# A decoder block on one core: value projection moved to the start, context rows and row parts moved forward

## The reference

```python
x = layernorm(x + self_attention(x))      # 32 heads of 16, ALiBi, causal; w_attn 512 x 1536, w_proj 512 x 512
x = layernorm(x + cross_attention(x, ctx))  # 32 query heads, 8 key heads of 128; keys and values from [ctx; x]
x = layernorm(x + ffn(x))                 # a permutation, 16 blocks of 32 -> 128 -> 32, the permutation back

qkv = x @ w_attn + b_attn                 # self-attention
scores = q @ k.T / 16 + slope[h] * (key - query), causal
out = softmax(scores) @ v @ w_proj + b_proj

k, v = kv @ Wk, kv @ Wv                   # cross-attention: 512 -> 8 x 128, kv = concat(ctx, x), then
q, k = rms_norm(q) * q_norm_w, rms_norm(k) * k_norm_w
```

## Time and profile before

| | |
|---|---|
| median of 3 runs | 845.17 us (844.33 to 846.02) |
| profiled execution, its own time | 845.65 us |
| its span, first to last instruction | 843.8 us |
| TensorE products busy | 826.2 us, 98% |
| VectorE busy | 547.2 us, 65% |
| ScalarE busy | 474.9 us, 56% |
| GpSimd busy | 521.9 us, 62% |
| granted TensorE clock, mean | 0.999 |
| DMA | 56.22 MB, mean 67 GB/s |

### The profile page before, as it was taken

The page is one execution under the profiler, slowest core; times in us unless marked ns, Lnnn a source line. Parts: engine busy times, 40 slices in busy tenths (PEclk is TensorE's granted clock), DMA queues, the critical chain, the costliest instruction groups (busy, mean ns, idle before and its releaser), DMA issues.

```text
span 843.8 us, 15130 instructions
## 1 busy us (share of the span) xinstructions
PE 826.2 (98%) x4851; PEld 694.6 (82%) x4851; DVE 547.2 (65%) x1507; ACT 474.9 (56%) x1006; POOL 521.9 (62%) x676
## 2 busy tenths in 40 slices
PE   7999999999999999999999999999999999999997
PEld 5777777777788888888888888888888888888874
DVE  4456566766355677667767676667666766677664
ACT  4666665566246656455555555556555555556554
POOL 3477876757336576766666756775676576636931
PEclk9999999999999999999999999999999999999999
DMA  6613223221141721112102112122121101100101
GB/s 202 197 51 113 80 72 114 63 72 56 50 138 51 243 80 46 51 60 67 50 19 87 27 61 68 37 68 68 37 68 68 37 2 24 58 0 1 26 1 50
DMA packets 48511, 56.22 MB, mean 67 GB/s; under 512 B 4671, under 2 KB 29773, under 8 KB 48461
## 3 DMA queue, kind: packets, MB, share of 16 engines
q1 hardware_dynamic: 48460, 55.59, 21.6%
HBM read 41.95 MB, written 13.63 MB: 66 GB/s over the span
## 4 chain that ended last, share of the span: by engine, by line
PE 61%; DVE 3%; ACT 2%; POOL 0%; issue 0%; POOLq 0%
PE bank L1534 15%; PE bank L48 11%; PE bank L50 11%; PE bank L49 11%; PE bank L1580 9%; PE bank L1524 1%; ACT prob L1349 1%; DVE x_mx L1420 1%; ACT prob L1724 1%; DVE pT_lo L1469 0%; PE bank L1849 0%; PE bank L1850 0%; PE bank L1881 0%; PE bank L1891 0%; PE bank L1890 0%
## 5 line engine op out<-in xcount | busy, mean ns | idle before, releaser
L1251 POOL TENSOR_SCALAR prob<-prob,x_rinv 128x768 f32<-128x768 f32 x124 | 112.5, 908 | 167.4 <-DVE x_rinv L1429 167.4
L1366 ACT ACTIVATE pT_hi<-bank 128x512 fp32r<-128x512 f32 x192 | 114.2, 597 | 90.3 <-PE bank L1580 89.9
L1349 ACT ACTIVATE prob<-bank,x_nm,q_rms 128x768 f32<-128x768 f32 x124 | 123.2, 994 | 47.1 <-DVE x_nm L1423 46.7
L1469 DVE TENSOR_TENSOR pT_lo<-bank,pT_hi 128x512 fp32r<-128x512 f32 x192 | 130.3, 679 | 5.1 <-ACT pT_hi L1366 3.7
L1420 DVE TENSOR_REDUCE x_mx<-bank 128x1 f32<-128x768 f32 x124 | 118.3, 954 | 22.0 <-PE bank L1534 21.7
L1580 PE MATMUL bank<-ident,prob 128*128 128x128 f32 x768 | 114.8, 272 | 2.1 <-POOL prob L1251 1.3
L1580 PEld LDWEIGHTS bank<-ident,prob 128*128 128x128 f32 x768 | 95.0, 140 | 14.1 <-POOL prob L1251 2.0
L48 PE MATMUL bank<-pT_hi,xv_hi 128*128 128x512 f32 x192 | 86.5, 450 | 1.2 <-DVE pT_lo L1469 0.9
L485 ACT ACTIVATE s_self<-s_self,nm_self 128x128 f32<-128x128 f32 (+1 forms) x128 | 57.1, 447 | 43.0 <-DVE nm_self L628 42.5
L50 PE MATMUL bank<-pT_hi,xv_lo 128*128 128x512 f32 x192 | 75.7, 394 | 0.0
L49 PE MATMUL bank<-pT_lo,xv_hi 128*128 128x512 f32 x192 | 75.4, 393 | 0.0
(11 more groups left out here) (233 smaller groups left out, 2047.8 us busy)
## 6 DMA issues: line engine op xcount, KB each, us to landing
wo_raw<-in_Wo SPq DMA_DIRECT2D x8, 1024.0 KB, 5.4
v_by_head<-v_st SPq DMA_DIRECT2D x12, 512.0 KB, 3.5
kT_by_head<-kT_st SPq DMA_DIRECT2D x12, 512.0 KB, 3.2
xk_raw<-kT_by_head SPq DMA_DIRECT2D x16, 384.0 KB, 3.2
xv_raw<-v_by_head SPq DMA_DIRECT2D x16, 384.0 KB, 3.2
wq_raw<-in_Wq SPq DMA_DIRECT2D x6, 1024.0 KB, 5.5
wq_raw<-in_w_attn SPq DMA_DIRECT2D x12, 256.0 KB, 4.3
xk_raw<-in_ctx SPq DMA_DIRECT2D x8, 256.0 KB, 2.6
```

Source lines behind the costliest of these rows:

```text
L1251: nc.gpsimd.tensor_scalar(prob[:, s, :], prob[:, s, :], rinv[:, s:s + 1], 1.0, ALU.mult, ALU.mult)\
L1349: nc.scalar.activation(prob[:, s, :].rearrange("p (a e) -> p a e", a=2), bank[:, at:at + 2, 0:HALF], ACT.Exp, bias=nm[:, s:s + 1], scale=q ...
L1366: nc.scalar.activation(pT_hi[:, a, :], bank[:, turn.bank[s, what, a], :], ACT.Copy)\
L1469: nc.vector.tensor_tensor(pT_lo[:, a, :], bank[:, turn.bank[s, what, a], :], f32(pT_hi[:, a, :]), ALU.subtract).then_inc(ring_out, 1)
```

## The change

1. Loads alternate: row group 0, weight block 0, row group 1 and so on; the first weight group is now the values' (`w_attn` 2), then queries, keys.
2. The values are projected first, in the fixed part, in groups of three products between the row transposes; queries and keys follow. V leaves the order list. The first context rows are loaded earlier and transposed into bank 1 between queries and keys.
3. Groups 3 and 5 are split by VectorE instead of GpSimd (8 subtractions); ScalarE's and VectorE's splits of groups 2 to 5 are placed one by one between queries and keys.
4. The first four row parts go beside the scores of quad 0, and four cycles (c = 1, 3, 5, 7) have one part less. So up to S(9) every CT, KT and KG sits at another place than before.

```diff
-    order = [("S", 0), ("W", 5), ("V", 0), ("E", (0, 0)), ("V", 1), ("E", (0, 1)), ("V", 2), ("E", (0, 2)), ("CT", 0), ("CX", 0), ("V", 3),
-             ("E", (0, 3)), ("R", (0, 0)), ("W", 6), ("R", (0, 1))]
+    order = [("S", 0)]
...
+    for i in range(QUAD):
+        parts(1)
+        order.append(("E", (0, i)))
+        if i % 2:
+            order.append(("R", (0, i // 2)))
+    order.append(("W", 6))
...
-        if c < NQ - 1:
+        if c not in (1, 3, 5, 7, NQ - 1):
             parts(1)
...
-        ON_VECTOR, ON_POOL = (0, 1, 2, 4, 6, 8), (3, 5, 7)
+        ON_VECTOR, ON_POOL = (0, 1, 2, 3, 4, 5, 6, 8), (7,)
...
-        before = {4: ("V", 0), 7: ("V", 3), 5: ("V", 1), 6: ("V", 2)}
-        place, quad, rows_over = {}, 0, {}
+        before = {4: ("K", 0), 7: ("K", 3), 5: ("K", 1), 6: ("K", 2)}
+        place, quad, rows_over = {("CT", 0): (1, None)}, 0, {}
...
-                name, g = (("w_attn", 0), ("w_attn", 1), ("w_attn", 2), ("Wk", 0), ("Wk", 1), ("Wv", 0), ("Wv", 1),
+                name, g = (("w_attn", 2), ("w_attn", 0), ("w_attn", 1), ("Wk", 0), ("Wk", 1), ("Wv", 0), ("Wv", 1),
                            ("w_proj", 0), ("Wq", 0), ("Wq", 1))[p]
                 for i in range(KT):
-                    if p > 0 and p - 1 in ON_VECTOR:
+                    if p == 0:
+                        sp.dma_start(x[:, i, :], d["x"].rearrange("b s d -> (b s) d")[tokens(i), :]).then_inc(x_in[i], 16)
+                    elif p - 1 in ON_VECTOR:
                         sp.wait_ge(w_los, KT * ON_VECTOR.index(p - 1) + i + 1)
...
             load_weights(1)
             sp.dma_start(proj_bias, d["b_proj"].rearrange("(a n) -> a n", a=1).to_broadcast([P, D])).then_inc(proj_bias_in, 16)
+            load_context(0)
             load_weights(2)
-            load_context(0)
...
-            late_lo(3)
-            late_lo(5)
...
+            for i in range(KT):
+                weights_hi(2, i)
+            queries_of(0)
+            queries_of(1)
+            weights_hi(3, 0)
+            weights_hi(3, 1)
+            queries_of(2)
+            weights_hi(3, 2)
+            weights_hi(3, 3)
+            weights_hi(4, 0)
+            queries_of(3)
+            context_hi(0)
+            for i in range(1, KT):
+                weights_hi(4, i)
+            act.wait_ge(nw_made, 2)
+            keys_of(0)
+            weights_hi(5, 0)
+            weights_hi(5, 1)
+            keys_of(1)
+            weights_hi(5, 2)
+            weights_hi(5, 3)
+            keys_of(2)
+            keys_of(3)
...
+            def values(i, j):
+
+                pe.wait_ge(xt_lo, j + 1)
+                pe.wait_ge(w_los, i + 1)
+                last = three_passes(nc, bank[:, 4 + j, :], xT_hi[:, i, tokens(j)], xT_lo[:, i, tokens(j)],
+                                    w_hi[:, 0, i, :], w_lo[:, 0, i, :], i == 0, i == KT - 1)
+                if i == KT - 1:
+                    last.then_inc(v_ps, 1)
+
+            pe.wait_ge(const, 4)
+            row_transposes(0)
+            row_transposes(1)
+            values(0, 0)
+            row_transposes(2)
+            for i, j in ((0, 1), (1, 0), (1, 1)):
+                values(i, j)
+            row_transposes(3)
+            for i, j in ((0, 2), (1, 2), (2, 0), (2, 1), (2, 2), (0, 3), (1, 3), (2, 3)):
+                values(i, j)
+            for j in range(TT):
+                values(KT - 1, j)
```

More of the change, by code:

```diff
@@ L536, in _, with keys_of @@
                     .then_inc(q_out, 1)
[L537 to L541, removed]
+            def keys_of(m):
                 act.wait_ge(qk_ps, KT + m + 1)
@@ L544, in _ @@
                                      scale=even[:]).then_inc(k_out, 1)
-                weights_hi(4, m)
-            act.wait_ge(zeros, 2)
-            for what, a in ORDER:
[L548 to L555, removed]
+            for i in range(KT):
[21 more added lines that the diff above has]
+            keys_of(3)
+            for what, a in ORDER:
+                if what == "CX":
                     context_hi(a)
@@ L676, in _, with odd_keys @@
                                         f32(xT_hi[:, :, tokens(j)]), ALU.subtract).then_inc(xt_lo, 1)
-            for p in range(2):
-                for i in range(KT):
-                    early_lo(p, i)
+                early_lo(0, j)
+            for i in range(KT):
+                early_lo(1, i)
+            def odd_keys(m):
+                dve.wait_ge(qk_ps, KT + m + 1)
+                dve.wait_ge(k_out, m + 1)
+                nc.vector.tensor_scalar(kT_odd[:, m, :], bank[:, 4 + m, :], cols[:, KT + m:KT + m + 1],
+                                        odd[:], ALU.add, ALU.mult).then_inc(k_odd_out, 1)
+            for i in range(KT):
+                early_lo(2, i)
             dve.wait_ge(col_out, 1)
@@ L685, in _ @@
             for i in range(KT):
[L686 to L692, removed]
+                early_lo(3, i)
+            early_lo(4, 0)
+            context_lo(0)
+            for i in range(1, KT):
+                early_lo(4, i)
+            odd_keys(0)
+            early_lo(5, 0)
+            early_lo(5, 1)
+            odd_keys(1)
+            early_lo(5, 2)
+            early_lo(5, 3)
+            odd_keys(2)
+            odd_keys(3)
             for what, a in ORDER:
@@ L796, in drained, with context_transposes, row_transposes @@
                     pe.wait_ge(vg_late, i[0] + 1)
-            pe.wait_ge(const, 4)
-            for j in range(TT):
+            def context_transposes(n):
+                pe.wait_ge(c_in, 16 * (n + 1))
+                if n > 0:
+                    drained("CT", n)
+                for i in range(KT):
+                    last = nc.tensor.transpose(bank[:, bank_of("CT", n), tokens(i)], c_raw[:, tokens(i)], ident[:])
+                last.then_inc(ct_ps, 1)
+            def row_transposes(j):
                 pe.wait_ge(x_in[j], 16)
@@ L870, in weigh_values @@
                 last.then_inc(o_ps, 1)
-            def context_transposes(n):
-                pe.wait_ge(c_in, 16 * (n + 1))
-                drained("CT", n)
-                for i in range(KT):
-                    last = nc.tensor.transpose(bank[:, bank_of("CT", n), tokens(i)], c_raw[:, tokens(i)], ident[:])
-                last.then_inc(ct_ps, 1)
             def key_transposes(n, g):
@@ L912, in _ @@
             for what, a in ORDER:
-                if what == "V":
-                    values(a)
-                elif what == "S":
+                if what == "S":
                     scores(a)
@@ L947, in _ @@
                         pe.wait_ge(s_out, QUAD * NQ)
[L948 removed]
+                        pe.wait_ge(w_los, 8 * KT)
                     for i in range(KT):
```

69 lines of the change are left out of this document (34 added, 35 removed).

## The result

The change makes the kernel slower: 852.42 us median of 4 executions (851.74 to 852.55), against 844.75 us for the kernel before in the same rounds (843.11 to 846.02). The ratio is 1.0083, with a 95% interval of 1.0071 to 1.0096. The profiled execution took 851.74 us with a span of 849.9 us, 6.1 more than before. Forecast were 848.6 us (844.0 to 851.2): the direction was right, the loss was more than twice what I summed, and the time lies outside the range.

What follows compares the result with a forecast made beforehand. TensorE was taken as the bound. A lead of -2.3 us, old waits gone at -1.9 and new waits of +7.7 gave +3.5 on the median of 845.17: 848.6 us, range 844.0 to 851.2.

Steps and rivals of the forecast that it cites:

- T(2,0): Transposes of quad 2's head 0: TensorE waits 2.7 us for VectorE's late result of the weighed values.
- S(5): Scores of quad 5: TensorE waits 1.1 us for a shift that VectorE makes after a context copy.
- T(4,2) with T(4,3): Transposes of quad 4's heads 2 and 3: waits of 2.3 us in all, behind GpSimd's late weight splits.
- KT(4,0): Key transposes in cycle 8: a wait of 0.8 us, between 0 and 1.0, for a late VectorE result.
- First product: At the start of the kernel: TensorE's first product begins at 6.65 us, not 9.28.
- New waits: the context row between weighing and transposes: Cycle 2: context copies and a shift delay VectorE's result that T(2,0) needs; a wait of 2.7 us.
- Smaller ones: Waits of 0.8 us near the scores of quad 1 (0 to 1.2), and 0.8 at KT(4,0) (0 to 1.0).
- Other cycles, stepped in the same manner, have none over 0.1: Remaining cycles of the loop: no new TensorE wait over 0.1 us.
- The lead: From the start to the scores of quad 1: the new order arrives there 2.3 us earlier.
- Hidden waits: Rival: queues keep ahead, T(2,0) waits under 0.3 us, waits left about 1.9; 842.9 us; chance 0.12.
- GpSimd catches up: Rival: the wait at T(2,0) lets GpSimd drain, so T(4,2) has none; +1.2, 846.4 us; chance 0.18.
- Slow clock for longer, by transposes: Rival: transposes among the first products put off the clock's rise to 19.4 us; 3.4 more, 852.0 us; chance 0.05.

Runs made afterwards that it cites:

- e1: Changed kernel with the context-row copies moved behind VectorE's result of the weighed values: 848.20 us, ratio 1.0036.
- e3: Changed kernel with GpSimd's split of the projection weights moved behind the scaling of quad 4's heads 2 and 3: 850.00 us, ratio 1.0054.
- e6: Changed kernel with one weight split (four VectorE subtractions) moved right behind the scores of quad 0: 853.43 us, ratio 1.0097.
- e12: e10 with the weight split that e6 moved placed behind the first shift of quad 1: 847.03 us over 12 executions, ratio 1.0018.
- e10: Changed kernel with the edits of e1 and e3, and row parts left out in cycles 1, 2, 4 and 6 instead: 844.61 us, ratio 0.9991.
- e4: Changed kernel with row parts left out in the even cycles 0, 2, 4, 6 instead of the odd ones: 851.20 us, ratio 1.0059.
- e2: Changed kernel with ten extra, unused products ahead of the transposes T(2,0): 850.38 us, ratio 1.0059.
- e8: Changed kernel with the edits of e4, e1 and e6 together: 848.11 us, ratio 1.0034.

## Why the prediction was right and wrong

**Right.** TensorE's waits decide, not its work, and the new short cycles lose more than the start gains. T(2,0), S(5), T(4,2) with T(4,3), and KT(4,0) were worked out step by step from rows 4 and 6 to 9, and each came within 0.2 us, by the mechanism named: 6.9 forecast, 7.25 measured; e1 and e3 take T(2,0)'s and T(4,2)'s away. First product: 6.65 forecast, 6.53 measured.

**The step that failed: "New waits: the context row between weighing and transposes".** It priced the 2.7 us at T(2,0) as a wait and nothing else. TensorE came out of it at 1.2 GHz for 3.4 us, a further 1.6. The profile before had no such wait after the start (its largest was 0.5), so no row said that it would come; but I had the price of the slow level from the start and looked for it only there. Without those 1.6 us the time would be near 850.8, inside the range. e1 removes 1.9 of the wait and the slow stretch, 3.5 together, and that is what lies between the profiled executions (851.74 and 848.20). The medians are 4.2 apart; the profiled execution of the change is the fastest of its four. Two of the other three show a mean clock of 0.996, which a second slow stretch would explain; but the third, at 852.33 us, shows 0.998 like the profiled one, and executions of the kernel before with 0.996 (844.4 to 845.0) are no slower than those with 1.000. So a second slow stretch is not shown, and the 0.7 stays open.

**The step "Smaller ones"** gave 0.8 for S(1) and T(0,1) with an upper bound of 1.2; they took 1.89. I priced GpSimd's scalings at their usual length though they stood beside VectorE's subtractions; e6 and e12 show that apart from them the scalings are short again.

**"Other cycles, stepped in the same manner, have none over 0.1"**: S(7) waits 0.78. CX(4), and the copy of values for the part ahead of it, are before E(6,3) on VectorE as CX(3) is before E(4,3); I stepped one and waved the other through. With T(1,3) and T(7,3) this term is 1.1.

**The lead** was mis-sized the other way, 2.3 against 3.35. I took the clock to rise as long after the start of the products as before, behind the second transposes (12.7); it rose near 10.3, 3.8 us after the first product. The prediction's own sentence for that case (2.5 us earlier is 1.2 more) gives 3.5.

Together: 3.5 - 1.05 + 1.6 + 1.09 + 1.1 + 0.35 (small excesses of the terms that held) = 6.6, against 6.1 in the span; the step from 6.1 to 7.7 lies in the choice of executions: the profiled one of before was 0.9 above its median (845.65 against 844.75), that of the change 0.7 below (851.74 against 852.42). One slip in the working: the terms at their low bounds add up to -1.2, not -1.4 (-3.5 - 1.9 + 2.7 + 1.0 + 0.5); nothing hangs on it.

**The rivals.** Hidden waits: refuted, T(2,0) waits 2.78. GpSimd catches up: refuted, T(4,2) waits 1.8 though T(2,0)'s wait lies ahead of it. Slow clock for longer, by transposes: refuted. The transposes at 7.95 stand in the middle of the slow stretch, and the clock rose 2.3 us after their start; those at 11.59 already ran at the higher level. The Trainium skill (TensorE: Matmul & The Clock Gate, Part 4: PE-mode transpose) says that the full clock does not engage for transposes; by that the rise would have been put off, and the trace does not bear it out for transposes mixed with products. That the time of this rival (852.0) is near what was measured is chance: the clock cost its time at another place, behind an idle TensorE.

## What to carry to other kernels

A stall of TensorE of some 2.6 us or more must be priced as its length plus a slow stretch that may follow (1.6 us here): read the granted clock after each wait in the profile, and put work that is already there, parts or even spare products, in front of the wait. When an order is shortened at one place, step every cycle by the same chain, and move the entry that is not urgent (here the context copy and the weight split) behind the one that frees what TensorE needs; with two such moves and other cycles made short, +7.7 us became level with the kernel before (e10). And before two engines are put to work side by side, look in the trace for a place where the same two instructions overlap: a length taken from where they don't is too short.

## What the runs showed of the hardware

**TensorE's clock can fall after one wait of 2.6 us in the middle of dense work.** It ran at half for 3.4 us in the profiled executions of the change, e3, e4 and e6 at the same place, and not when the wait was 0.7 (e1) or filled with products (e2). The Trainium skill (TensorE: Matmul & The Clock Gate, Part 1: The HAM clock gate) says that idleness brings the lower clock back; e1 and e2 agree. It is not certain each time: behind a wait of 2.8 us at S(1) it fell in e6 and not in e8, and the executions of e4 and e12 fall in two groups. Waits of 1.3 and 1.7 us in the change had no slow stretch behind them.

**VectorE's subtraction and GpSimd's scaling slow each other down.** Beside W(6), scalings of 0.37 and 0.48 us took 1.32 and 1.42, and the four subtractions 3.19 instead of 2.49; in e12 two biases on GpSimd took 1.52 instead of 0.89. The Trainium skill (SBUF — State Buffer, SBUF: two separate sides) says that VectorE and GpSimd share a pair of ports, for which a VectorE instruction with two inputs in SBUF contends with a GpSimd instruction that reads SBUF, and that the first to start keeps it for its whole length. The subtraction has two such inputs and the scaling reads SBUF, and e6 and e12 agree in that the times grow only where the two overlap; which port was held, no trace here shows.
